# A decoder layer with 16 experts: adding the routed results ahead of the shared ones in the last chunk, and storing that chunk batch by batch

## The reference, cut to what matters

```python
shared_out = silu(h @ shared_w1) * (h @ shared_w2) @ shared_w3        # h = layernorm(x), width 1024
gates = one_hot(top2(sigmoid(h @ router_w) + expert_bias)) * scores   # two gates of a token are not zero
for e in range(16):
    routed += (silu(h @ w1[e]) * (h @ w2[e]) @ w3[e]) * gates[:, e]
out = x + shared_out + routed
```

## Time and profile before

| What | us |
|---|---|
| median of 3 runs | 638.5 |
| lowest and highest of them | 636.83, 640.86 |
| the profiled execution: its own time | 641.78 |
| the profiled execution: its span in the trace | 640.5 |
| PE busy in the span | 556.2 |
| DVE busy in the span | 312.3 |

### The profile page before, as it was taken

One profiled execution on the slowest core, in us unless ns is written; L12 is line 12 of the kernel. 1 busy time (PEld: TensorE's weight loads), 2 busy tenths in 40 slices (PEclk: granted clock), 3 DMA queues, 4 the chain that ended last, 5 costly groups with the idle time before them and its releaser, 6 DMA issues.

```text
span 640.5 us, 9893 instructions
## 1 busy us (share of the span) xinstructions
PE 556.2 (87%) x3274; PEld 336.2 (53%) x3274; DVE 312.3 (49%) x677; ACT 227.2 (35%) x422; POOL 221.5 (35%) x449
## 2 busy tenths in 40 slices
PE   4933979859989979599999989997999999999995
PEld 2522435326555546565567537454566666655454
DVE  4634778884698754756415453210222223222263
ACT  6311564633735535346431410100333333332110
POOL 2421465655725434222101004663233433334000
PEclk9975897979989979799979999998999999999999
DMA  7697559436522329800006925222233223321711
GB/s 206 197 189 117 94 106 221 102 68 184 103 61 47 134 65 160 233 1 1 1 0 220 349 88 182 83 84 83 67 91 92 84 88 91 88 83 58 270 67 65
DMA packets 62144, 72.39 MB, mean 113 GB/s; under 512 B 14768, under 2 KB 55216, under 8 KB 60560
## 3 DMA queue, kind: packets, MB, share of 16 engines
q1 hardware_dynamic: 58304, 61.37, 38.9%
q0 software_dynamic: 3792, 10.39, 4.6%
HBM read 45.31 MB, written 26.03 MB: 111 GB/s over the span
## 4 chain that ended last, share of the span: by engine, by line
PE 38%; issue 19%; DVE 13%; DMA 12%; POOL 11%; ACT 5%; SPq 1%; POOLq 0%; DVEq 0%; ACTq 0%
PE ps L515 10%; DMA x_slots<-XN,slot_i 7%; POOL y_rows L1450 7%; PE ps L526 5%; PE ps L377 4%; PE ps L319 3%; PE ps L365 2%; ACT prob L1188 2%; DVE nmax L794 2%; PE ps L346 2%; PE ps L439 2%; PE ps L460 2%; PE ps L448 2%; DMA pack_k<-qk_parts 1%; PE ps L505 1%
## 5 line engine op out<-in xcount | busy, mean ns | idle before, releaser
L794 DVE TENSOR_REDUCE nmax<-ps 128x8 f32<-128x1024 f32 x64 | 77.8, 1216 | 51.6 <-PE ps L346 51.3
L570 PE MATMUL ps<-W,xt 128*128 x188 | 90.0, 602 | 0.7 <-ACT xt L1278 0.4
L1188 ACT ACTIVATE prob<-ps 128x1024 f32<-128x1024 f32 x64 | 65.4, 1022 | 34.2 <-PE ps L365 34.2
L1450 POOL DMA_INDIRECT y_rows<-yo,goes_to x47 | 45.8, 975 | 90.5 <-DVE yo L1001 90.5
L994 DVE TENSOR_TENSOR sa<-sa,ps 128x256 f32<-128x256 f32 x47 | 19.8, 421 | 97.7 <-ACT sa L1285 97.7
L515 PE MATMUL ps<-xT,W1s 128*128 128x512 f32 x128 | 62.1, 609 | 0.9 <-DVE yo L1001 0.9
L526 PE MATMUL ps<-W3s,hTs 128*128 128x256 f32 x256 | 58.7, 391 | 2.6 <-DVE hTs L927 2.6
L515 PE MATMUL ps<-xT,W2s 128*128 128x512 f32 x128 | 60.2, 592 | 0.0
L927 DVE TENSOR_TENSOR hTs<-sil,ps 128x512 f32<-128x512 f32 x32 | 22.0, 687 | 71.4 <-PE ps L515 59.5
L526 PEld LDWEIGHTS ps<-W3s,hTs 128*128 128x128 f32 x256 | 49.9, 196 | 12.1 <-DVE hTs L927 5.1
L1271 ACT ACTIVATE sil<-ps 128x512 f32<-128x512 f32 x32 | 19.1, 597 | 99.5 <-PE ps L515 78.8
(11 more groups left out here) (182 smaller groups left out, 868.9 us busy)
## 6 DMA issues: line engine op xcount, KB each, us to landing
W<-in_L_ffn_routed_w_dram SPq DMA_DIRECT2D x12, 1024.0 KB
qk_parts<-part SPq DMA_DIRECT2D x28, 256.0 KB, 3.7
pack_q<-qk_parts SPq DMA_DIRECT2D x48, 128.0 KB, 3.8
pack_k<-qk_parts SPq DMA_DIRECT2D x48, 128.0 KB, 4.3
xg<-x_slots SPq DMA_DIRECT2D x47, 129.0 KB
x_slots<-zero SPq DMA_DIRECT2D x11, 512.0 KB, 10.2
yg<-y_rows SPq DMA_DIRECT2D x4, 1024.0 KB, 8.5
X<-in_x_dram SPq DMA_DIRECT2D x4, 512.0 KB, 7.7
```

The costliest lines, as they stand in the source:

```text
L570: r = t.matmul(ps[:, 2 + p, :], xt[:, p, k, :], W12[:, ds(e, 1), k, :].rearrange("p o f -> p (o f)"), start=(k == 0), stop=(k == KT - 1))
L794: v.tensor_reduce(nmax[:, s % 4, a, :, :], ps[:, 0:2, :].rearrange("p m (h t) -> p m h t", h=4), AX_X, ALU.max, negate=True).then_inc(maxe ...
L1188: a.activation(prob[:, n:n + 2, :], ps[:, 2:4, :], ACT.Exp, scale=HD ** -0.5).then_inc(exped, 1)
L1450: g.indirect_dma_start(out=y_rows, out_offset=bass.IndirectOffsetOnAxis(ap=goes_to[:, n:n + 1].bitcast(U32), axis=0), in_=yo[:, p, :], in_ ...
```

## The change

In the tail, DVE adds the routed results of all batches ahead of the last downs. The table `ROUTED_WITH_UP` says how many batches are added behind gate_up(3, f): 0, 0, 2, 2, 2, 3, 3, 2, so 14. Batches 14 and 15 are added ahead of add_shared(3, 0) and of add_shared(3, 1). The waits for `rows_back[c]` stand ahead of the first batch of each chunk, and each add_shared of chunk 3 has a wait for `routed_added` in addition. In `sync_program`, chunks 0 to 2 are stored as before; chunk 3 is stored by four DMAs of one batch (128 KB) each, released by `shared_added`.

```diff
+ROUTED_WITH_UP = (0, 0, 2, 2, 2, 3, 3, 2)
...
+            b = 0
             for f in range(FS):
                 gate_up(NC - 1, f)
-                if f >= 3:
-                    c = (f - 3) // 2
-                    if f % 2:
-                        v.wait_ge(rows_back[c], 16)
-                        v.wait_ge(shared_added, CB * (c + 1))
-                    for j in range(2 * ((f - 3) % 2), 2 * ((f - 3) % 2) + 2):
-                        add_routed(c * CB + j)
+                for _ in range(ROUTED_WITH_UP[f]):
+                    if b % CB == 0:
+                        v.wait_ge(rows_back[b // CB], 16)
+                    if b == 0:
+                        v.wait_ge(shared_added, CB * (NC - 1))
+                    add_routed(b)
+                    b += 1
             for j in range(CB):
+                if b < NB:
+                    add_routed(b)
+                    b += 1
+                v.wait_ge(routed_added, 2 * ((NC - 1) * CB + j + 1))
                 add_shared(NC - 1, j)
-                if j < 2:
-                    if j == 0:
-                        v.wait_ge(rows_back[2], 16)
-                        v.wait_ge(shared_added, CB * 3)
-                        add_routed(2 * CB + 2)
-                    else:
-                        add_routed(2 * CB + 3)
-            v.wait_ge(rows_back[3], 16)
-            for j in range(CB):
-                v.wait_ge(shared_added, 3 * CB + j + 1)
-                add_routed(3 * CB + j)
...
-            for c in range(NC):
+            for c in range(NC - 1):
                 put_out(c)
-            q.wait_ge(out_stored, 16 * NC)
+            for b in range((NC - 1) * CB, NB):
+                q.wait_ge(shared_added, b + 1)
+                q.dma_start(ov[:, b, :], X[:, b, :]).then_inc(out_stored, 16)
+            q.wait_ge(out_stored, 16 * (NC - 1 + CB))
```

## The result

| | before | after |
|---|---|---|
| median of 22 runs each, in turns | 640.71 | 637.24 us |
| lowest and highest | 636.59, 646.76 | 632.5, 642.05 |
| profiled execution: time, span | 641.78, 640.5 | 638.05, 636.8 |

The ratio, taken from the fast runs of each kernel, is 0.9937 with a 95% interval of 0.9913 to 0.9961: 4.0 us less, between 2.5 and 5.6; the two medians lie 3.5 us apart. The forecast gain of 4.8 us (a ratio of 633.7 / 638.5 = 0.9925) lies in the interval; the forecast time of 633.7 us does not fit, and its range of 631.2 to 636.6 missed the measured 637.24. So the difference came out about as worked out, and the level did not.

The account below looks back on a forecast made before the run. It took PE's chain, then DVE's last adds and the last store's landing, as the bound in the tail. Adds 3.67 plus landing 1.12, other terms 0, gave 4.8 us off 638.5: 633.7 us, range 631.2 to 636.6.

Parts of the forecast that it names:

- What bounds the tail: Behind PE's last matmul stand one add_shared, 3.67 us of adds on DVE, and the landing of a 512 KB store.
- the forecast term: On DVE, the eight routed adds behind the last add_shared leave the path: 3.67 us.
- The landing: Last store, 128 KB in place of 512 KB: landing goes from 2.9 to 1.78 us, 1.12 us less.
- The first rival: Last store's landing hardly depends on its size: 2.4 to 2.9 us, so 634.3 to 634.8 us; chance 0.20.
- The cover in the ups: DVE's three batches behind gates 5 and 6 take 3.36 of 3.43 us: cost 0, upper end 0.1 us.
- my sign against it: No DVE idle time ahead of gates 6 and 7, and PE's downs over 28.6 us behind the first up.
- The second and third rivals: Rows back too late for gate 2, 636.0 us, chance 0.05; DVE becomes the bound of the last ups, chance 0.03.
- the third rival: DVE bounds the last ups: add pairs dearer by d make gate 7 late by 6d - 0.14; chance 0.03.
- The waits: Added waits on DVE for routed_added and earlier one for rows_back cost 0; bounds for routed_added -0.05 and 0.1 us.
- The sum: Whole tail: 3.67 + 1.12 - 0 - 0 = 4.79, so 4.8 us off the execution.
- The fourth rival: Whole-kernel runs lie 4.0 us apart, so the median could come out at 632 or 636; no chance of its own.

Follow-up runs that it names:

- adds alone: Changed kernel with chunk 3 stored by one DMA of 512 KB behind the last add_shared; median 636.66 us, ratio 0.9895, tail 46.1 us.
- the stores alone: Kernel before with adds in the old order, but chunk 3 stored batch by batch; median 639.14 us, ratio 0.9971, tail 48.6 us.

## Why the prediction was right in the tail and wrong in the level

*What bounds the tail.* Right. DVE was the end of the chain, and taking its eight adds off moved the end by 3.7 us (adds alone: 46.1 against 49.8), the forecast term being 3.67.

*The landing.* Right, and a little better than forecast: 1.7 us measured where I had 1.78, so the smaller store gives 1.2 us in place of 1.12. The first rival, that size hardly counts, is out by three sizes on one line.

*The cover in the ups.* Right: three batches behind a gate left the gates 3.43 us apart, and the price of a fourth batch came out as 0.60 + n x 0.92 gives it. One half of my sign against it did come, no idle time ahead of gates 6 and 7; the other did not, since PE's downs start 28.59 us behind the first up in both kernels (619.27 - 590.68, 620.38 - 591.79). The second and third rivals have no line in any profile: the four read-backs again landed in 5.3 to 11.8 us, and no add of the changed kernel took over 485 ns although the stores now ran beside other adds:

```profile
L1005 DVE SCALAR_TENSOR_TENSOR X<-yg,gate,X x16: 476/479/480, 603.1 to 624.5; 128x256 f32<-128x256 f32 x16
L1008 DVE SCALAR_TENSOR_TENSOR X<-yg,gate,X x16: 483/485/485, 603.6 to 625.1; 128x256 f32<-128x256 f32 x16
```

The lateness in the third rival was worked out too low, for it counted only gates 6 and 7. Two adds of a batch that cost more than 1.42 us together would also make gates 3, 4 and 5 late (0.60 + 2 x 1.42 = 3.44 us); no run came near that.

*The waits.* Right at 0 for the adds: the first add behind gate 2, with two waits between, starts 0.60 us after it. Not quite for the sums, where a second wait now stands ahead of each. The last sum starts 634.57 - 620.38 = 14.19 us behind the start of the downs, before 633.38 - 619.27 = 14.11, and the first sum is later by the same 0.08 us. The six profiles with the second wait and the downs started as before have 14.18 or 14.19 us, and the four without that wait 14.11 or 14.12. On the chain that ended last, 0.09 us now pass between the end of PE's piece and the sum, with the wait for PE (L931) as a step of its own (above). Before, it was 0.02 us:

```profile
633.36 0.02 issue
633.38 0.03 DVE X L932
```

*The sum.* The tail fell from 49.8 to 45.0 us, 4.8 us, in both pairs of profiles. That it fits to 0.1 us is in part luck: the landing gave back some 0.08 us more than I had, and the waits took 0.08.

*The step that failed* is "the same 4.8 us come off the median: 638.5 - 4.8 = 633.7 us", with "the scatter of medians of three, about 1.5 us". It took the median of three runs as the level of the kernel. That level is 640.71 over 22 runs, and 642.03, 642.14 and 640.61 in the later sets: the three runs were 2.2 us low. Of the 22 runs only four are at 638.5 or under, so a median of three draws from them is this low about once in eleven times, 3 x (4/22)^2 - 2 x (4/22)^3 = 0.09. The one further number I had, the profiled execution at 641.78, stood above all three of them, and I used it for the sum but not to widen the level. The scatter had to be counted twice, once for the median that I started from and once for the one I forecast. The fourth rival had said that scatter could swamp the gain; the range did not give it enough room. The other line of the sum, from the profiled execution, 641.78 - 4.8 = 637.0 us, lies 0.24 us from the measured median, and that is luck too, since it starts from a single execution.

The median over 22 runs less 4.8 is 635.9 us, inside the range. The rest, up to 637.24, I put down to scatter of the changed kernel, whose second set had 635.16; no run isolates it. Its 22 runs lie in two groups, ten up to 636.09 and twelve from 637.0 on, so the median sits at the edge of the upper group, and two runs more in the lower one would have brought it to 636.1 or less.

## What to carry to other kernels

Look at what stands behind the last matmul. Whatever does not need its result belongs ahead of it, in the idle time of its engine, and the fit can be read off as (first start + n x step) against the period of the producer; here three of 0.92 us fitted into 3.43, and four, behind two gates, cost 1.6 us. The last store should carry only what the last result made: here its landing took 1.3 us plus its bytes at some 330 GB/s.

When the gain is under 1% and single executions scatter by more, give the time of the stretch the change touches, which repeats to 0.1 us, and take the level of the whole from as many runs as there are, with its own error in the range.

A wait that is taken away far from the end can come back as another: look at what PE waits for next before the gain is counted.

## What the runs showed that I had not expected

The tail repeats to 0.1 us over three profiles of the kernel before, while its start moves by 4.75 us (588.30 to 593.05): in these profiles the scatter arises ahead of it.

The first of the four small stores landed in 2.6 and 2.4 us in the two profiles of the changed kernel, and in 1.9 to 3.5 us in the four variants of it that have the same four stores; the other three landed in 1.7 us each time, and all four did in the run with the stores alone. It is not on the path, and its cause stays open. The listing from 621 to 626 us of the first profile:

```profile
out_dram<-X SPq DMA_DIRECT2D x1, 128.0 KB, 2.6
```

Taking away a wait of PE that the trace lists at 0.8 us was worth 1.15 us, twice: start to start, the downs came 1.0 us earlier behind the last up, not 0.85, and the last ups came (591.79 - 588.78) - (590.51 - 588.55) = 1.05 us earlier behind the routed matmuls, not 0.82. The piece of PE behind the wait also gets 0.1 us shorter: the 64 matmuls of the downs take 13.98 us in place of 14.08, and the first four matmuls of the ups 1.88 in place of 1.99. Together that is 1.1 us in the one case and 1.16 in the other, which is the 1.15 to the rounding of spans to 0.1 us.
